# The last edge pass of a four-layer graph network: half of its table rows looked up by one-hot products from SBUF instead of gathered from DRAM

## The reference

```python
h = jnp.concatenate([x[row], edge_attr], axis=1)
h = jax.nn.relu(h @ W1a + b1a) @ W1b + b1b
sums = jax.ops.segment_sum(h, col, num_segments=n_nodes)
agg = sums / jnp.clip(counts, 1.0)[:, None]
z = jnp.concatenate([x, agg, u[batch]], axis=1)
return jax.nn.relu(z @ W2a + b2a) @ W2b + b2b
```

## Time and profile before

| what | value |
|---|---|
| median of three runs | 9446.55 us |
| the profiled execution | 9442.52 us |
| its span, first to last instruction | 9440.8 us |
| TensorE busy (matmuls) | 6822.4 us, 72% |
| VectorE busy | 4912.0 us, 52% |
| GpSimd busy | 3361.7 us, 36% |
| ScalarE busy | 2485.4 us, 26% |
| mean granted TensorE clock | 0.777 |

### The profile page before, as it was taken

How to read it: one execution, slowest core, us unless ns; L and a number is a source line. 1 busy time by engine, 2 the same in 40 slices (tenths; PEclk the granted TensorE clock), 3 DMA queues, 4 the chain that set the end, 5 groups by cost and what they waited for, 6 DMA issues and landing times. The chain is left out here.

```text
span 9440.8 us, 104137 instructions
## 1 busy us (share of the span) xinstructions
PE 6822.4 (72%) x31843; PEld 4196.1 (44%) x31843; DVE 4912.0 (52%) x13495; ACT 2485.4 (26%) x5860; POOL 3361.7 (36%) x3682
## 2 busy tenths in 40 slices
PE   5777777775566669920688699999996666666665
PEld 4555555453122224410677544444454444444444
DVE  7777777775599970079899600000013333333333
ACT  0222222222467730020588400000001111111111
POOL 0777777776410000000000000000006777777771
PEclk9766676776689999965899899999996555555556
DMA  3333333335965548859466488887884444444443
GB/s 101 105 104 104 104 102 105 104 104 201 390 207 164 168 138 305 293 230 428 158 216 214 134 296 268 279 278 258 296 271 112 104 103 103 104 103 103 103 101 36
DMA packets 904492, 1675.69 MB, mean 177 GB/s; under 512 B 103880, under 2 KB 640093, under 8 KB 840344
## 3 DMA queue, kind: packets, MB, share of 16 engines
q1 hardware_dynamic: 766728, 1335.70, 44.3%
q0 software_dynamic: 134208, 330.54, 11.3%
q10 hardware_dynamic: 3024, 2.84, 0.1%
HBM read 1384.71 MB, written 283.96 MB: 177 GB/s over the span
## 5 line engine op out<-in xcount | busy, mean ns | idle before, releaser
L1659 POOL DMA_INDIRECT arena<-table,idx x1664 | 1628.6, 979 | 514.9 <-issue 409.5
L697 POOL DMA_INDIRECT bucketed<-arena,wide x1563 | 1518.6, 972 | 715.9 <-issue 706.5
L1628 POOL DMA_DIRECT2D table<-wide x13 | 9.7, 744 | 4450.9 <-DVE wide L1552 4450.9
L1702 PE MATMUL psum<-arena 128*128 128x128 f32 x3328 | 930.7, 431 | 747.5 <-DVE arena L1713 566.0
L532 PE MATMUL psum<-blank 128*128 128x120 bf16 (+1 forms) x5856 | 1211.7, 322 | 24.1 <-PEq L88 18.7
L1702 PEld LDWEIGHTS psum<-arena 128*128 128x128 f32 x3328 | 731.1, 306 | 1072.2 <-DVE arena L1713 780.0
L1501 PE MATMUL psum<-arena,h 128*128 128x512 f32 (+1 forms) x2548 | 1049.3, 571 | 15.9 <-DMA arena<-adjacency 13.6
L841 PE MATMUL psum<-arena 128*128 128x512 bf16 x2304 | 697.3, 438 | 430.1 <-DVE arena L789 262.8
L1720 DVE TENSOR_TENSOR arena<-arena 128x256 f32<-128x256 f32 x832 | 357.1, 429 | 1141.4 <-DMA arena<-table,idx 1110.4
L594 PE MATMUL psum<-arena 128*113 128x177 bf16 x1568 | 536.4, 342 | 419.9 <-ACT wide L616 379.1
L1680 ACT ACTIVATE arena<-arena 128x256 f32<-128x256 f32 x832 | 346.4, 416 | 1753.6 <-DVE arena L1720 1753.5
(11 more groups left out here) (337 smaller groups left out, 9597.5 us busy)
## 6 DMA issues: line engine op xcount, KB each, us to landing
arena<-adjacency SPq DMA_DIRECT2D x294, 1024.0 KB, 4.8
arena<-adjacency SPq DMA_DIRECT2D x98, 1568.0 KB, 7.7
adjacency<-wide SPq DMA_DIRECT2D x588, 256.0 KB, 2.3
arena<-adjacency SPq DMA_DIRECT2D x196, 640.0 KB, 3.9
arena<-adjacency SPq DMA_DIRECT2D x147, 768.0 KB, 4.2
arena<-bucketed POOLq DMA_DIRECT2D x208, 528.0 KB, 6.1
arena<-bucketed SPq DMA_DIRECT2D x832, 128.0 KB, 2.2
arena<-adjacency SPq DMA_DIRECT2D x49, 1792.0 KB, 6.8
```

Of the source, the lines that this page charges most:

```text
L697: e.indirect_dma_start(bucketed, bass.IndirectOffsetOnAxis(ap=places[k][0:size, c:c + 1], axis=0), rows[k][0:size, c, :], None).then_inc(s ...
L1659: e.indirect_dma_start(ring[:, k, c, 0:D], None, table, bass.IndirectOffsetOnAxis(ap=idx[:, k, c:c + 1], axis=0)).then_inc(s_got[k], 16)
L1702: last = e.matmul(psum[:, k, 0:D], lhsT=onehot[:, k, c, :], rhs=extra[:, k, c, :], start=c == 0, stop=c == PAIR - 1)
```

## The change

The pairs are split in halves: the first 416 ("near") and the last 416 ("far"). Far pairs are gathered as before. For near chunks the table row of each edge comes from TensorE. As edges are sorted by source tile inside a destination tile, a chunk meets few source tiles. A meeting of a chunk and a source tile is one product: a one-hot of the chunk's source numbers against that tile's 128 nodes (made by VectorE, 128x128), times the tile's 128x128 piece of the table, which is still in `wide2`. The products of one chunk add up in one of four banks, into which ScalarE has copied the chunk's edge rows; then ScalarE rectifies the bank into a stage and stores four chunks at once to `near_rows` in DRAM.

The meetings are a list in DRAM, `look_chunk` and `look_tile`, with the last meeting of each chunk in `chunk_end`. Its length is fixed at `LOOKS` = 3248; what lies past the real meetings of the near half has a chunk number that is capped, and is executed without effect.

- In the preparation, 28 more relayed steps make codes and positions for the 49x49 buckets. In `build_adjacency` GpSimd scatters them, 98 scatters of 49 elements. Beside the GIN sum, ScalarE and VectorE turn the marks into lists (`near_tables`). Beside the maximum pass, ScalarE and TensorE transpose the source numbers into `near_src`.
- `edge_pass` becomes two blocks. The first walks the 416 far pairs; with each of the first 406, TensorE and VectorE do eight meetings. VectorE also rectifies the far messages now, in place, and GpSimd gathers straight by `src_i`; `idx` and the `keep_awake` products are gone. Slots for the far pair's one-hots and banks are four deep, those for meetings eight.
- The second block walks the 416 near pairs: SyncE loads `near_rows`, VectorE builds one-hots of destinations and adds to `h`, TensorE multiplies.

The core of the diff:

```diff
+NEAR_PAIRS = PAIRS // 2
+NEAR = NEAR_PAIRS * PAIR
+FAR_PAIRS = PAIRS - NEAR_PAIRS
+LOOKS = -(-(NEAR + BUCKETS_49 + 2) // 16) * 16
+PER_PAIR = 8
+QUAD = 4
...
                     e.tensor_scalar(src_i[:, :], src_i[:, :].bitcast(fp32), -1.0, 0.0, op0=ALU.add, op1=ALU.max)
+                    e.wait_ge(s_marks, 32)
+                    for b in range(TILES):
+                        e.indirect_dma_start(look_marks, bass.IndirectOffsetOnAxis(ap=look_to[:, b:b + 1], axis=0),
+                                             look_code[:, b:b + 1], None).then_inc(s_look_mark, 16)
+                        e.indirect_dma_start(chunk_marks, bass.IndirectOffsetOnAxis(ap=chunk_to[:, b:b + 1], axis=0),
+                                             chunk_code[:, b:b + 1], None).then_inc(s_chunk_mark, 16)
...
             with nc.Block() as block:
                 @block.gpsimd
                 def _(e):
+                    for n in range(FAR_PAIRS):
+                        k = n % DEEP
+                        if n >= DEEP:
+                            e.wait_ge(s_pe, n - DEEP + 1)
+                        for c in range(PAIR):
+                            chunk = (NEAR_PAIRS + n) * PAIR + c
+                            e.indirect_dma_start(ring[:, k, c, :], None, table,
+                                                 bass.IndirectOffsetOnAxis(ap=src_i[:, chunk:chunk + 1], axis=0)).then_inc(s_got[k], 16)
...
                 @block.scalar
                 def _(e):
+                    def prepare(c):
+                        g = c // QUAD
...
+                        e.copy(bank(c), near_edge[:, g % 3, c % QUAD * P:(c % QUAD + 1) * P]).then_inc(s_clear, 1)
+                    def evict(c, end):
+                        g = c // QUAD
+                        e.wait_ge(s_looked, end)
...
+                        e.activation(stage[:, g % 2, c % QUAD * P:(c % QUAD + 1) * P], bank(c), ACT.Relu).then_inc(staged.sem, 1)
+                        e.wait_ge(staged.sem, staged.at + c + 1)
...
+                    for g in range(quads):
+                        _, end = nc.values_load_multi_w_load_instructions(
+                            end_of[0:1, g * QUAD:(g + 1) * QUAD], engines=(ENG.Activation,), min_val=1, max_val=LOOKS,
+                            skip_runtime_bounds_check_because=reason)
+                        for k in range(QUAD):
+                            c = g * QUAD + k
+                            evict(c, end[k])
+                            if c + 4 <= NEAR:
+                                prepare(c + 4)
+                        e.dma_start(near_rows[:, g * QUAD * D:(g + 1) * QUAD * D], stage[:, g % 2, :]).then_inc(s_near_out[g % 2], 16)
+                        if g + 4 < quads:
+                            e.wait_ge(s_clear, 15 + QUAD * (g + 2))
+                            load_edges(g + 4)
+                            load_rows(g + 4)
...
                 @block.tensor
                 def _(e):
+                    def look_up(i, chunk, tile):
+                        e.wait_ge(look.sem, look.at + i + 1)
+                        e.matmul(flat[:, ds((chunk & 3) * 512 + 2048, P)], lhsT=hot[:, i % 8, :], rhs=table_in[:, ds(tile * P, P)],
+                                 start=False, stop=True, skip_group_check=True).then_inc(s_looked, 1)
+                    for n in range(FAR_PAIRS):
+                        if n * PER_PAIR < LOOKS:
+                            here = slice(n * PER_PAIR, (n + 1) * PER_PAIR)
+                            _, chunk = nc.values_load_multi_w_load_instructions(
+                                chunk_of[0:1, here], engines=(ENG.PE,), min_val=16, max_val=NEAR + 16, skip_runtime_bounds_check_because=reason)
+                            _, tile = nc.values_load_multi_w_load_instructions(
+                                tile_of[0:1, here], engines=(ENG.PE,), min_val=0, max_val=TILES - 1, skip_runtime_bounds_check_because=reason)
+                            for k in range(PER_PAIR):
+                                look_up(n * PER_PAIR + k, chunk[k], tile[k])
+                        e.wait_ge(s_hot, n + 1)
+                        e.wait_ge(s_msg, n + 1)
+                        if n >= 4:
+                            e.wait_ge(s_add, n - 2)
+                        for c in range(PAIR):
+                            last = e.matmul(psum[:, n % 4, 0:D], lhsT=onehot[:, n % 4, c, :], rhs=ring[:, n % DEEP, c, :], start=c == 0, stop=c == PAIR - 1)
+                        last.then_inc(s_pe, 1)
...
                 @block.vector
                 def _(e):
+                    def looks(n):
...
+                            if k % 2 == 0:
+                                e.wait_ge(s_clear, chunk[k + 1])
+                                if i >= 8:
+                                    e.wait_ge(s_looked, i - 6)
+                            e.tensor_scalar(hot[:, i % 8, :], rows[:, ds((chunk[k] & 15) * P, P)], tile_first[:, ds(tile[k], 1)], None,
+                                            op0=ALU.is_equal).then_inc(look.sem, 1)
...
+                        message(n)
+                        if n * PER_PAIR < LOOKS:
+                            looks(n)
+                        rectify(n)
...
+                        if n > 0:
+                            add(n - 1, held_tile)
+                            if n + 3 < FAR_PAIRS:
+                                one_hots(n + 3)
```

More of the change, by code:

```diff
@@ L1636, in edge_pass, with slots @@
         def edge_pass():
[L1637 to L1639 removed]
+            nonlocal at_arena
+            at_arena = 0
+            def slots(n, k):
+                return room(n * k).rearrange("p (k w) -> p k w", k=k)
+            ring = slots(PAIR * P, DEEP).rearrange("p k (c w) -> p k c w", c=PAIR)
```

383 lines of the change are left out of this document (295 added, 88 removed).

## The result

The changed kernel takes 9368.07 us (median of 4 runs, 9366.17 to 9369.43) against 9452.88 for the kernel before: a ratio of 0.9915, 95% interval 0.9903 to 0.9927. It is 85 us faster. The forecast was 9615, slower. The time lies inside the range, the sign is wrong.

The account below looks back on a forecast made before the run. GpSimd's gathers were taken to bound the last edge pass. First block 1949 + 60 + 10, second 300, start 13, block change 3: 2335 against 2175, +160; with 8 ahead, +168 on 9442.5, plus 4: 9615 us, range 9290 to 9880.

Parts of the forecast that it names:

- the forecast case: First block: TensorE's own stream sets the pace at 4.45 to 5.3 us per pair; total 9615 us, chance 0.38.
- the sum for one pair on TensorE: First block: register loads, eight meetings and the pair's two products, without overlap in TensorE's stream, 4.8 us per pair.
- The break-even named in the prediction: First block: at 4.38 us per pair, all else fixed, the pass takes as long as before; each 0.1 us is worth 41.
- The pair's own products, 0.45 us, and the register loads, 1.4: First block, TensorE per pair: two products, partly behind the next loads, 0.45 us; two register loads at 0.70, 1.4 us.
- The meetings, 8 x 0.37: First block, TensorE per pair: eight meetings at 0.37 us, between stream 0.33 and half-clock data side 0.43; 2.96 us.
- The second block, 0.72 us a pair: 416 near pairs at 0.72 us each, 300 us; bounds 0.55 and 0.95, 230 and 395 us.
- The ScalarE stalls, 60 us: First block: ScalarE just under TensorE's pace and four banks a short buffer; 60 us allowed for stalls.
- Ahead of the pass, 8 us: Preparation: 28 chained steps, 6 us, with a barrier and four more iotas 8 us; the scatters of marks nothing.
- A: First block: TensorE's stream cheap at 3.7 us, VectorE the bound at 4.0 per pair; total 9290, faster; chance 0.32.
- B: First block: GpSimd and VectorE block each other, VectorE 5.3 us per pair; +203, total 9818, slower; chance 0.12.
- C: First block: ScalarE the bound of real meetings, 6.6 to 7.5 us per four chunks; middle 9805, slower; chance 0.13.
- The test named in the prediction: First block: TensorE's idle time before the meetings' products ends at "issue" or its own sequencer, not at VectorE.

Follow-up runs that it names:

- pe_third: Changed kernel, TensorE loading the eight tile numbers twice in each of 406 batches: 10518 us, ratio 0.9770 to the kernel before, slower kind of chip.
- off_by_one: Changed kernel with both meeting lists laid 4 bytes further on, so register loads start unaligned: 10473 us in one run, +1105 over 9368.
- near_light: Changed kernel without ScalarE's loads of edge and source rows for near chunks after the first sixteen: 9345 us in one run, -23 against 9368.
- dve_third: Changed kernel with a third register load, on VectorE, in each of 406 batches: 10468 us, ratio 0.9721 to the kernel before, slower kind of chip.
- bank_list: Changed kernel with TensorE's bank numbers from their own list, one register instruction less per meeting: 10207 us, ratio 0.9468 to the kernel before, slower kind of chip.
- no_gather: Changed kernel without the far half's 832 GpSimd gathers: 10267 us in one run, against 10259 for the changed kernel on that slower kind of chip.
- spread8: Changed kernel with 2048 meeting places, 256 batches of eight spread evenly over the first block's pairs: 9077 us, ratio 0.9590 to the kernel before.
- trim: Changed kernel with the meeting list cut to 2048 places, 256 batches instead of 406: 10074 us, ratio 0.9375 to the kernel before, slower kind of chip.
- spread5: Changed kernel with 2080 meeting places, five with each of 416 pairs: 10270 us, ratio 0.9553 to the kernel before, slower kind of chip.

## Why the prediction was wrong

**The place and the kind were right.** TensorE's own instruction stream sets the first block, as the forecast case had it, and its price is register loads plus meetings. pe_third (+0.625 us a pair for a load of 0.59) shows it, and off_by_one (+2.70 for 2 x 1.35) agrees. The step that failed is the sum for one pair on TensorE, 4.8 us. Measured are 4.25 with filler and 4.49 with real meetings ((8298.1 - 7162.2) / 253, from ScalarE's first and last rectification), 4.40 over all. The break-even named in the prediction, 4.38, has the 60 us of stalls beside it, so 4.25 is what it is to be held against.

- **The pair's own products, 0.45 us, and the register loads, 1.4.** Together 1.85, measured 1.58. The loads measure 0.59 + 0.06 of issue each, 1.30, at the lower bound given and not at 0.70; the products cost not 0.45 but what is left, under 0.3, because they run beside the first load. "Nothing of this overlaps inside TensorE's own stream" was the false sentence; the 0.45 took only a part of the overlap in. 0.27 x 406 = 110 us.
- **The meetings, 8 x 0.37.** Measured 2.72, so 0.34. I had mixed the stream (0.33) with the data side at half clock (0.43). The clock went up to 0.94 to 1.00, and pe_third shows that at 0.82 the data side costs nothing either. 0.24 x 406 = 97 us.
- **The second block, 0.72 us a pair.** Measured 0.60: the one-hots' starts run from 8963.4 to 9213.6. In the timeline VectorE's two instructions go every 0.53 us, and every eighth pair takes 0.97. TensorE's four weight loads also go at 0.53 a pair, so which of the two sets it is not shown. It is the lower end of the range given, near the 0.54 worked out for VectorE. 50 us:

```profile
L2036 DVE TENSOR_TENSOR arena<-iota,dst_f x416: 411/416/427, 8963.4 to 9213.6; 128x256 f32<-128x256 f32 x139
```

- **The ScalarE stalls, 60 us.** The real batches are 253 x 0.24 = 61 us dearer than filler. The amount was right, the cause only for a third (near_light).
- **Ahead of the pass, 8 us.** Measured 24: sized too low, against the sum.

The three first errors are 257 us, against a forecast of +160 for the pass: that turns it into -100. None was large in itself, but 406 repetitions make 41 us of every 0.1 us, and all lay on the same side. In each a value above the nearest row was chosen: 0.70 for a load of eight values where the row has 0.597, 0.37 for a meeting whose stream had been put at 0.33, and 0.72 for the second block where VectorE's two instructions made 0.54.

**The rivals.** A (VectorE the bound) gave 9290 at 4.0 us, the nearest of the four cases, 78 us too low; its mechanism is refuted, as TensorE leads. With its 4.0 it had VectorE's stream nearly right (4.09 by dve_third and by bank_list), but TensorE's, at 3.7, half a microsecond too cheap. That its time came nearest is in part luck. B is refuted: GpSimd's gathers keep their 944 ns and VectorE's one-hots and rectifications their 286 ns beside each other, and no_gather changes nothing (286 ns there too). A rectification that starts at 8601.21, 0.05 us into a gather, takes 0.29 us and the gather 0.95. The Trainium skill (SBUF — State Buffer, Who interferes with whom) has GpSimd and a 2-port VectorE instruction exclude each other; no run here shows such an exclusion, and none shows which mode these instructions ran in. Their lines in after (ns min/median/max):

```profile
L1841 POOL DMA_INDIRECT arena<-table,src_i x832: 938/944/7147, 7147.6 to 8955.0; - x167
```

```profile
L1979 DVE TENSOR_SCALAR arena<-wide,tile_first x3248: 273/286/530, 7160.3 to 8944.5; 128x128 f32 x192
```

```profile
L1959 DVE TENSOR_SCALAR arena<-arena x416: 273/286/530, 7162.2 to 8961.1; 128x256 f32<-128x256 f32 x139
```

C is refuted: ScalarE's load of four values takes 314 ns, a tenth of the 3.14 us it was bounded by, and ScalarE idles 574.6 us for TensorE. The floor of about 600 ns that the Trainium skill (DMA: Bandwidth & Descriptors, Latency and other measured facts) gives for `tensor_load` agrees with eight values (589), not with four (314).

The test named in the prediction for "TensorE's stream sets it", idle time that ends at "issue" and not at VectorE, held in the row of the weight loads (493.3 of 618.3 us) and seemed to fail in the row of the products (393.9 us put down to VectorE's one-hots). The second row is the wrong one to trust: in the timeline the one-hot named had been done 2.6 us before.

## What to carry to other kernels

When a block repeats a small instruction sequence hundreds of times, price the sequencer's work (register loads, register instructions, waits) from the rows nearest in kind and size, take these as they stand, and ask of every pair of neighbours whether the engine's queue lets them run side by side. In a list of waits an engine's own register loads can be put down to another engine whose result had long been there: compare when that result was done with when the waiting engine's last register load ended. Which of two streams of nearly equal length leads is then confirmed by adding a known cost to each (one load on TensorE +0.63 us a pair, on VectorE +0.50). And a work list cut to its real length gains more when its batches are spread over the block (spread8 -291 us) than when the filler is merely dropped (trim -194), provided that each register load keeps an aligned start. The two ran on different kinds of chips, which makes the difference look larger than it is. On spread8's kind trim's 160 pairs without a batch might go at the 2.6 us of the kernel before instead of 2.9, and trim would gain some 50 us more (an estimate); the other 50 of the 97 us between them are then the spreading.

## What the runs showed of the hardware that was not expected

- A register load's time depends on where it starts. Eight int32 values from a multiple of 32 bytes take 0.59 us on TensorE and 0.60 on VectorE; from 4 bytes further on 1.94 and 1.84. Four values from a multiple of 16 bytes take 0.31 on ScalarE. Five take 0.59 from a multiple of 16 bytes and 1.18 to 1.25 from elsewhere (spread5). Other counts and starts were not run.
- TensorE's next register load starts before the products issued ahead of it have run (8600.1 against 8600.2 for their weight loads), so a pair's two products followed by register loads add under 0.3 us.
- Chips differ where indirect transfers set the pace: the kernel before took 9453 to 9457 us in one place and 10743 to 10764 in the others, with gathers of the same 0.94 us on GpSimd, 3.10 against 2.61 us a pair. The size of this change's gain hangs on it (0.9915 or 0.9536). What differs in those chips was not found.
